# Residual rows stored ahead of the experts' sums, and the scan's states walked up and down

## The reference

```python
mod = (silu(c) @ wmod).reshape(16, 6, 1, 256)          # sa, ca, ga, sb, cb, gb
ga, gb = keep_away_from_zero(ga), keep_away_from_zero(gb)
h = layernorm(x) * (1 + ca) + sa
x = x + ga * attn(h)
h = layernorm(x) * (1 + cb) + sb
x = x + gb * ffn(h)                                    # the output

def attn(x):                                           # 512 inner channels, 16 states
    xn = layernorm(x) * norm_scale + norm_bias
    xb, z = split(xn @ W_in)
    xb = silu(conv3(xb) + conv_b)
    dt = softplus(xb @ W_dt + b_dt)
    A, B, C = -exp(A_log), xb @ W_B, xb @ W_C          # B, C: 512 tokens x 16 states
    for t in range(512):                               # for every state n
        s[:, n] = exp(dt[t] * A[:, n]) * s[:, n] + dt[t] * xb[t] * B[t, n]
        y[t] = sum over n of s[:, n] * C[t, n]
    return x + ((y + D * xb) * silu(z)) @ W_out

def ffn(x):                                            # 16 experts, 4 of them per token
    w = route(x)                                       # 512 x 16 weights, 12 of each row zero
    return sum over e of w[:, e] * (silu(x @ gate[e].T) * (x @ up[e].T)) @ down[e].T
```

## Time and profile before

| | us |
|---|---|
| median of 3 runs (2824.08 to 2827.97) | 2825.69 |
| the profiled execution, its own time | 2827.94 |
| its span, first to last instruction | 2826.1 |
| PE, DVE, POOL, ACT busy | 2394.2, 2427.1, 2238.7, 1566.2 |
| mean granted TensorE clock | 0.929 of full speed |

### The profile page before, as it was taken

The page is one execution under the profiler, slowest core; times in us unless marked ns, Lnnn a source line. Parts: engine busy times, 40 slices in busy tenths (PEclk is TensorE's granted clock), DMA queues, the critical chain, the costliest instruction groups (busy, mean ns, idle before and its releaser), DMA issues.

```text
span 2826.1 us, 29195 instructions
## 1 busy us (share of the span) xinstructions
PE 2394.2 (85%) x9004; PEld 1680.1 (59%) x9004; DVE 2427.1 (86%) x2450; ACT 1566.2 (55%) x2961; POOL 2238.7 (79%) x1563
## 2 busy tenths in 40 slices
PE   3445698998989899998989999898989989898799
PEld 1212466666756666665666667566666756566678
DVE  2678899989989898999999898998989999898932
ACT  3555666566556656655665665566565556655311
POOL 1577888888888888888888888888888888887922
PEclk7677899989989898998989899898999999999999
DMA  4699999999999999999999999998999999999921
GB/s 111 183 226 230 228 235 244 231 235 236 236 232 238 236 234 231 239 235 232 237 240 235 229 236 234 232 238 231 234 235 229 238 231 239 235 240 223 257 69 49
DMA packets 354510, 626.18 MB, mean 222 GB/s; under 512 B 51489, under 2 KB 162081, under 8 KB 354353
## 3 DMA queue, kind: packets, MB, share of 16 engines
q0 software_dynamic: 72960, 243.30, 45.3%
q1 hardware_dynamic: 281392, 381.01, 43.0%
HBM read 379.25 MB, written 10.06 MB: 138 GB/s over the span
## 4 chain that ended last, share of the span: by engine, by line
PE 40%; DVE 24%; issue 12%; POOL 8%; ACT 8%; DMA 7%; SPq 1%; DVEq 0%; POOLq 0%; ACTq 0%
DVE hbank L705 13%; PE wbank L477 13%; PE mbank L489 6%; PE wbank L419 4%; PE wbank L505 4%; PE wbank L379 4%; POOL unit L1177 4%; PE wbank L367 3%; DMA w_all<-w_scratch 2%; DMA gsum<-unit 2%; PE wbank L502 2%; DMA w_scratch<-rows_out 2%; DVE unit L719 2%; ACT z L828 2%; DVE act L683 2%
## 5 line engine op out<-in xcount | busy, mean ns | idle before, releaser
L1177 POOL TENSOR_TENSOR unit<-dtx,b_bc 128x1024 f32<-128x1024 f32 x512 | 1359.5, 2664 | 7.5 <-DMA b_bc<-bc_scratch 4.3
L705 DVE TENSOR_TENSOR_SCAN hbank<-hbank,unit 128x1024 f32<-128x1024 f32 x512 | 1173.2, 2291 | 104.0 <-ACT hbank L1007 90.7
L1007 ACT ACTIVATE hbank<-dt,a_neg 128x512 f32<-128x512 f32 x1024 | 669.0, 681 | 334.3 <-DVE unit L719 300.1
L489 PE MATMUL mbank<-down_t,act 128*128 128x256 f32 x2048 | 532.9, 400 | 60.8 <-POOL act L1145 34.4
L1189 POOL DMA_DIRECT2D gsum<-unit x448 | 451.3, 1007 | 161.9 <-DVE unit L719 74.8
L719 DVE TENSOR_TENSOR unit<-hbank,c_bc 128x1024 f32<-128x1024 f32 x448 | 545.4, 1217 | 21.7 <-DMA c_bc<-bc_scratch 1.4
L1145 POOL TENSOR_TENSOR act<-act,w_all 128x512 f32<-128x512 f32 x256 | 360.9, 1410 | 254.3 <-DVE act L683 230.9
L477 PE MATMUL wbank<-h_t,gate_t 128*128 128x256 f32 x2048 | 496.8, 386 | 24.4 <-DVE act L683 13.0
L489 PEld LDWEIGHTS mbank<-down_t,act 128*128 128x128 f32 x2048 | 399.9, 199 | 165.8 <-issue 62.3
L477 PE MATMUL wbank<-h_t,up_t 128*128 128x256 f32 x2048 | 486.9, 381 | 11.8 <-DVE gz L587 10.2
L477 PEld LDWEIGHTS wbank<-h_t,gate_t 128*128 128x128 f32 x2048 | 387.3, 192 | 128.4 <-DVE act L683 27.4
(11 more groups left out here) (121 smaller groups left out, 2394.9 us busy)
## 6 DMA issues: line engine op xcount, KB each, us to landing
gsum<-unit POOLq DMA_DIRECT2D x448, 512.0 KB, 7.6
b_bc<-bc_scratch SPq DMA_DIRECT2D x512, 256.0 KB, 6.3
c_bc<-bc_scratch SPq DMA_DIRECT2D x512, 256.0 KB, 5.6
w_all<-w_scratch SPq DMA_DIRECT2D x256, 256.0 KB, 5.0
ht<-in_L_attn_x_dram SPq DMA_DIRECT2D x16, 512.0 KB, 8.8
w_out<-in_L_attn_W_out_dram SPq DMA_DIRECT2D x16, 512.0 KB, 10.1
ht<-in_L_attn_x_dram POOLq DMA_DIRECT2D x16, 512.0 KB, 10.3
out_dram<-xt SPq DMA_DIRECT2D x16, 512.0 KB, 3.3
```

What stands on the lines that cost most here:

```text
L489: m = eng.matmul(mbank[:, u * H:(u + 1) * H], act[:, (n - 1) % MOE_RING, j, u * P:(u + 1) * P], down_t[:, e, :], start=(e == 0 and u == 0) ...
L705: eng.tensor_tensor_scan(h, h, unit[:, g % RING, :, :].rearrange("p a t -> p (a t)"), 0.0, ALU.mult, ALU.add).then_inc(scanned, 1)
L1007: eng.activation(hbank[g % HB][:, a, :], dt[:, 2 * q + a, :], ACT.Exp, scale=a_neg[:, 2 * q + a, n:n + 1]).then_inc(decayed, 1)
L1177: eng.tensor_tensor(unit[:, g % RING, :, :], dtx[:, 2 * q:2 * q + 2, :], b_bc[:, s:s + 1, :].to_broadcast([P, 2, T]), ALU.mult).then_inc(d ...
```

## The change

The row x1 is stored to the output as soon as it is there (`store_x1`, one DMA of 512 KB on SP, at moment 27 of the slot). A half's experts' sum is then only multiplied by gb, from `mbank` straight into `xt` (over x1), and POOL issues a DMA that adds this half of `xt` onto the output in DRAM (256 KB, two per row, `accum_op=ALU.add`). DVE's multiplication waits until the store of x1 has landed (`x1_out`). And the 16 states of a pair are now taken upward and downward in turn (`state_at`), with the order reversed from row to row; a row of B or C that still lies in its ring from the last units before the turn is used again and not loaded (`rows_held`).

```diff
+        def state_at(g):
+            row, pair, u = g // NU, g % NU // NS, g % NS
+            return u if (row + pair) % 2 == 0 else NS - 1 - u
+
+        def rows_held(ring):
+            slots, table = [(None, 0, -1)] * ring, []
+            for g in range(NG):
+                row, n = g // NU, state_at(g)
+                s = (n - NS * (row % 2)) % ring
+                what, loads, reader = slots[s]
+                fresh = what != (row, n)
+                slots[s] = ((row, n), loads + fresh, g)
+                table.append((s, loads + fresh, fresh, reader))
+            return table
...
-                         ("project", behind, 4, 15, 24), ("stats", behind, 5, 20, 26),
+                         ("project", behind, 4, 15, 24), ("stats", behind, 5, 20, 26), ("store_x1", behind, 1, 27, 27),
...
-                        eng.tensor_tensor(sums, sums, gb_row[:, :].rearrange("p (a h) -> p a h", a=1).to_broadcast(
-                            [P, TT // 2, H]), ALU.mult).then_inc(moe_v, 1)
-                        need.wait_ge(moe_v, 2 * row + h + 1)
-                        eng.tensor_tensor(xt[:, row % 2, tiles, :], sums, xt[:, row % 2, tiles, :],
-                                          ALU.add).then_inc(moe_out, 1)
+                        need.wait_ge(x1_out, 16 * (row + 1))
+                        eng.tensor_tensor(xt[:, row % 2, tiles, :], sums, gb_row[:, :].rearrange(
+                            "p (a h) -> p a h", a=1).to_broadcast([P, TT // 2, H]), ALU.mult).then_inc(moe_out, 1)
...
+                    for h in range(2):
+                        if s == (EP + 1, E)[h]:
+                            tiles = slice(h * TT // 2, (h + 1) * TT // 2)
+                            need.wait_ge(moe_out, 2 * row + h + 1)
+                            need.wait_ge(x1_out, 16 * (row + 1))
+                            eng.dma_start(out[row].rearrange("(t p) h -> p t h", p=P)[:, tiles, :],
+                                          xt[:, row % 2, tiles, :], accum_op=ALU.add).then_inc(row_out, 16)
...
+            def store_x1(row):
+                x1_ready(need, row)
+                eng.dma_start(out[row].rearrange("(t p) h -> p t h", p=P), xt[:, row % 2, :, :]).then_inc(x1_out, 16)
+                yield
...
             def load_b(g):
+                s, _, fresh, reader = b_rows[g]
+                if not fresh:
+                    return
...
-                    if s == E:
-                        need.wait_ge(moe_out, 2 * (row + 1))
-                        eng.dma_start(out[row].rearrange("(t p) h -> p t h", p=P),
-                                      xt[:, row % 2, :, :]).then_inc(row_out, 16)
```

More of the change, by code:

```diff
@@ L233, in build @@
         summed = [sem(f"summed{k}") for k in range(2)]
-        etanhed, weighted, down_done, moe_v, moe_out = (
-            sem(n) for n in ("etanhed", "weighted", "down_done", "moe_v", "moe_out"))
+        etanhed, weighted, down_done, moe_out, x1_out = (
+            sem(n) for n in ("etanhed", "weighted", "down_done", "moe_out", "x1_out"))
         work = Banks(wbank, [sem(f"work{k}_full") for k in range(3)], [sem(f"work{k}_free") for k in range(3)])
@@ L301, in last_streams @@
             plan = [("mix1", last, 4, 5, 5), ("project", last, 4, 6, 6),
-                    ("stats", last, 5, 6, 8), ("turn", last, 4, 16, 18), ("load_gb", last, 1, 21, 26),
+                    ("stats", last, 5, 6, 8), ("store_x1", last, 1, 10, 10), ("turn", last, 4, 16, 18), ("load_gb", last, 1, 21, 26),
                     ("pick", last, 5, 16, 16), ("weigh", last, 2, 24, 25)]
@@ L708, in times_c @@
             def times_c(g):
-                s = g % C_RING
-                need.wait_ge(c_in[s], 16 * (g // C_RING + 1))
+                s, loads, _, _ = c_rows[g]
+                need.wait_ge(c_in[s], 16 * loads)
                 need.wait_ge(scanned, g + 1)
@@ L933, in project @@
                     if row >= 2:
-                        need.wait_ge(row_out, 16 * (row - 1))
+                        need.wait_ge(row_out, 32 * (row - 1))
                         need.wait_ge(rnorm_p, 4 * (row - 1))
@@ L1002, in decay @@
                 g, a = i // 2, i % 2
-                q, n = g % NU // NS, g % NS
+                q, n = g % NU // NS, state_at(g)
                 need.wait_ge(dt_cut, g // NS + 1)
@@ L1170, in drive @@
             def drive(g):
-                row, q, s = g // NU, g % NU // NS, g % B_RING
-                need.wait_ge(b_in[s], 16 * (g // B_RING + 1))
+                row, q = g // NU, g % NU // NS
+                s, loads, _, _ = b_rows[g]
+                need.wait_ge(b_in[s], 16 * loads)
                 need.wait_ge(dtx_made, 2 * row + q + 1)
@@ L1299, in load_b @@
             def load_b(g):
+                s, _, fresh, reader = b_rows[g]
+                if not fresh:
+                    return
+                n = state_at(g)
                 need.wait_ge(bc_out, 16 * (g // NU + 1))
[L1301 to L1304, removed]
+                if reader >= 0:
+                    need.wait_ge(driven, reader + 1)
+                eng.dma_start(b_bc[:, s, :], bc_dram[g // NU, n:n + 1, :].to_broadcast([P, T])).then_inc(b_in[s], 16)
             def load_c(g):
+                s, _, fresh, reader = c_rows[g]
+                if not fresh:
+                    return
+                n = NS + state_at(g)
                 need.wait_ge(bc_out, 16 * (g // NU + 1))
-                if g >= C_RING:
-                    need.wait_ge(c_scaled, g - C_RING + 1)
-                eng.dma_start(c_bc[:, g % C_RING, :], bc_dram[g // NU, NS + g % NS:NS + g % NS + 1, :].to_broadcast(
-                    [P, T])).then_inc(c_in[g % C_RING], 16)
+                if reader >= 0:
+                    need.wait_ge(c_scaled, reader + 1)
+                eng.dma_start(c_bc[:, s, :], bc_dram[g // NU, n:n + 1, :].to_broadcast([P, T])).then_inc(c_in[s], 16)
             def load_w(row, s):
@@ L1403, in _ @@
             older.rest()
-            need.wait_ge(row_out, 16 * NB)
+            need.wait_ge(row_out, 32 * NB)
 _INS = ['L0_attn_x', 'L0_attn_norm_scale', 'L0_attn_norm_bias', 'L0_attn_W_in', 'L0_attn_conv_w', 'L0_attn_conv_b',
```

3 lines of the change are left out of this document (2 added, 1 removed).

## The result

The changed kernel takes 2837.13 us (median of 4 runs, 2834.17 to 2842.16) against 2825.69: ratio 1.0043, 95% interval 1.0028 to 1.0058. It is slower by 0.43%, where I forecast 0.2% faster; the time lies just outside my range of 2803 to 2836. The profiled execution took 2834.17 us, its span is 2832.4.

The account below looks back on a forecast made before the run. No single engine bounds it; the chain of waits runs through DVE, POOL and DMAs. Terms -8.4 + 4.0 - 3.0 + 1.4 - 1.1 + 1.0 = -6.1 us gave 2821.8, adjusted to 2819.5 against median 2825.69; range 2803 to 2836.

Parts of the forecast that it names:

- Half 1, POOL: Adding DMA's issue in POOL's gapless run: 1.1 us less 0.79 covered, +0.31 per slot, +4.0 us in 13 slots.
- the cover: Wait for w_all before POOL's weighting, 0.79 us per slot, taken to hide part of half 1's issue.
- Half 0, DVE: Removing L696 at the slot's end brings scan, next slot and PE 0.6 us forward: 14 slots, -8.4 us.
- 0 (POOL sets it instead): Lower bound of half 0's DVE saving: at DVE's hand-over to PE, POOL sets the pace and nothing is gained.
- Half 0, POOL: Adding DMA's issue ahead of the addition at 1388.21: 1.1 us hidden by POOL's idle 1.56 us, cost 0.
- SP: Output store no longer delays w_scratch's store: weights up to 3.7 us earlier, w_all's wait gone; -3.0 us in the last slot.
- The store of x1: Issued ahead of the next row's ht load, which lands 1.7 us later; counted 0, bounds 0 and +1 per slot.
- The turns: 112 fewer loads, net -50 us of engine time with the adding DMAs, over units 13 to 20; counted 0.
- Rival 4: The transfers were the bound: half of the 50 us of engine time would give 2795 us; chance 0.06.
- Last slot and tail: Earlier weights -3.0, transfer before the last gsum addition +1.4, shorter experts' chain -1.1, final adding DMA +1.0 us.
- Rival 1: POOL's issue at half 1 becomes the bound: at issue cost p = 2.0 us, 2837.5 us; chance 0.22.
- Rival 2 (the clock): PE's 1.2 GHz stretch at the weights' routing takes half 0's gain: +2.3, 2828 us; chance 0.18.

Follow-up runs that it names:

- no_add1: Changed kernel without half 1's adding DMA, its output lacking that half's gated sums; 2807.79 us, 0.9943 of the kernel before.
- one_pass: Kernel before with DVE's gating and residual passes made one, the residual left out of the output; 2826.58 us, ratio 1.0010.
- no_add0: Changed kernel without half 0's adding DMA, its output lacking that half's gated sums; 2829.85 us, 1.0023 of the kernel before.
- turns_late_out: Kernel before with state order and held rows alone, plus SP's output store moved behind w_scratch and the first w_all loads; 2806.79 us, 0.9922.
- turns: Kernel before with only the alternating state order and the held rows of B and C, output path unchanged; 2813.76 us, 0.9964.
- late_x1: Changed kernel with the store of x1 issued some 30 us later in SP's order; 2836.9 us, 1.0042 of the kernel before.
- late_both: Changed kernel with half 1's adding DMA (rows 0 to 13) and the store of x1 both issued later; 2814.97 us, 0.9966 of the kernel before.
- adds: Changed kernel with rising state order and every B and C row loaded, keeping stored residual and adding DMAs; 2834.26 us, 1.0035 of the kernel before.

## Why the prediction was wrong, step by step

**Half 1, POOL: +0.31 us a slot forecast (+4.0 in 13 slots), +1.05 measured (+13.7)**, from scan 12 to scan 18, before to after. This is the first of the two steps that failed. The issue was sized at 1.1 us between 0.9 and 1.9; its row is 1.2 to 2.1 us, and its price, in POOL's run as in the slot, 1.9 (1.93 us, scan 12 to 18, no_add1 to after). The rows of L1173 (duration ns min/median/max; idle before it; landing):

```profile
L1173 POOL DMA_DIRECT2D out_dram<-xt x32: 1202/1277/2142, 405.5 to 2826.8; - x32
...
  issue: 7.2, 12
...
DMA to landing us min/median/max: 4.4/6.0/9.6
```

And the cover was looked up on the wrong path. I set the issue against `w_all`'s wait on the way to unit 17; it reaches the scans earlier, through L1117, ACT's queue and the gates, at unit 15, where `w_all` covers nothing. With 1.9 for 1.1 my own sum gives 1.9 - 0.79 = 1.1 a slot, nearly the measured number, but by luck: by the table, what stands against the issue is DVE's saving at 12-13 (0.64), which I had at nothing, and only 0.11 at 16-17, on `w_all`'s path. The kernel before already showed ACT waiting at L834's place for L1098 in all 13 slots (14.8 us): an edge without slack, which I had not followed.

**Half 0, DVE: -0.6 us a slot forecast (-8.4 in 14), -0.07 measured (scan 28 to 4, in one_pass and after alike), and nothing in the time of one_pass.** This is the second step that failed. I took PE's wait of 1.62 us for proof that the edge was worth its 0.6. It was shortened by 0.73, and at the next edge of the same chain, POOL's weighting, PE waited 0.72 longer. The bound "0 (POOL sets it instead)" was the right one.

**Half 0, POOL: 0 forecast, 0.2% measured** (no_add0), in the tail and at half 1 of the next slot; nothing at its own place.

**SP: the mechanism was right.** The store no longer stands before `w_scratch`, the waits for `w_all` are gone, and that is worth 7 us (turns_late_out to turns, 0.4% by the ratios). In the changed kernel it hardly shows (16-17 is 0.11 us shorter, 0.54 in no_add1), since unit 15 is late before unit 17 can be early.

**The store of x1: 0 forecast, right by the result** (late_x1); 7 us once the other bound is gone (late_both). **The turns: 0 forecast**; -11.5 alone, 0 or a little more than 0 in this kernel (adds 2834.26, after 2837.13). Rival 4 was right in part: loads left out, an estimated 94 us of engine time by the prediction's price, are worth 11.5 us alone. By the Trainium skill's DMA: Bandwidth & Descriptors, section Queues, rings and completion order, a DMA engine takes the queues it has work for in turn. That fewer loads on one queue would then speed the other fits only weakly: in the turns' trace the median landing of a `gsum` addition went from 7.6 to 7.4 us, while `w_all`, on the loads' own queue, went from 5.0 to 4.5.

**Last slot and tail: -3.0 + 1.4 - 1.1 + 1.0 = -1.7 forecast, +2.5 measured** (-1.1 and +3.6). The last slot gave 1.1 us where I had SP's 3.0. In the tail +1.3 stood against +3.6. By the chains of before and after, the last `gsum` addition takes 6.9 us to land instead of 5.4, +1.5 for my +1.4; it is issued 0.8 later, counted at nothing, for of the 1.50 us that POOL idled before it 0.52 are left; the experts' chain is 0.5 shorter for my 1.1; and the end, from DVE's first instruction on the last half, is 6.6 us instead of 4.8, +1.8 for my +1.0. The last addition in the chain of waits, before, then after:

```profile
2688.71 5.36 DMA gsum<-unit
```

```profile
2692.17 6.91 DMA gsum<-unit
```

Timeline of POOL after, at the last additions and at the end:

```profile
2689.55 0.87 POOL L1217 DMA_DIRECT2D gsum<-unit  x1 [1.36 <-DMA gsum<-unit]
2690.13 1.53 POOL L1173 DMA_DIRECT2D out_dram<-xt  x1
2692.17 0.90 POOL L1217 DMA_DIRECT2D gsum<-unit  x1 [0.52 <-DMA gsum<-unit]
...
2826.81 1.21 POOL L1173 DMA_DIRECT2D out_dram<-xt  x1 [3.08 <-DVE xt L715]
```

From the last issue to the end of the span are 5.6 us. The Trainium skill's formula for a DMA that POOL issues (DMA: Bandwidth & Descriptors, section Anatomy of one DMA), quoted in the prediction, gave an estimated 2.6; the trace does not agree.

**The rivals.** Rival 1 named the mechanism, the place and a time of 2837.5 at p = 2.0 us. Both numbers came out, the time by luck: it took the path over `w_all`, its 6.2 us at half 0 were wrong, and it kept the -8.4 of DVE. I gave it 0.22 because I placed two packets per partition nearer to one than to four; the row's median, 1.28 us, lies nearer to four (1.50) than to one (0.89), and the pause ahead of it was in none of my rows. Rival 2 (the clock) is refused: it had no change, and the mean granted clock is higher after (0.934) than before (0.929) although the kernel is slower. What the filling matmuls gained was 0.16% (0.07 to 0.25%).

## What to carry to other kernels

Before an instruction is added to a queue, follow who waits for what stands behind it, all the way to the engine that sets the pace, and look in the list of waits for edges that wait every time: a microsecond there cost a full microsecond of slot here, on an engine that idles for a fifth of the span. A wait that an edit removes is a gain only if the next wait on the same chain ends earlier; look for the second-latest input before counting it. Two edits may each be worth 7 to 12 us alone and nothing behind a third that delays an earlier point of the same slot, so time them apart.

## What the runs showed of the hardware

POOL's issue of an adding DMA of 256 KB into DRAM took 1.2 to 2.1 us and 1.9 in all in a run of POOL work without a gap, where a 512 KB addition into SBUF with half the packets per partition takes 0.9. It landed after 4.4 to 9.6 us. TensorE's clock could be brought from 0.95 to 0.98 of full speed over 2130 us by matmuls in its waits, for 0.16% of the time.

One row of DVE that no edit touched got dearer: `r_w<-r_cut,r_s` of the routing took 6.1 us in 16 runs of it before, 12.1 after, 11.6 in adds and 6.9 in turns; it accounts for most of what DVE's saving fell short of. One of them in the kernel after, and the drive that POOL was then running:

```profile
2105.37 2.64 POOL L1205 TENSOR_TENSOR unit<-dtx,b_bc 128x1024 f32<-128x1024 f32 x1
...
2106.52 1.58 DVE L677 SCALAR_TENSOR_TENSOR r_w<-r_cut,r_s 128x64 f32<-128x64 f32 x1
```

All 11 long ones after (0.35 to 1.59 us) start while POOL runs L1205 and end 0.09 us after it does; the other 5 overlap it by at most 0.02 us and take 0.22. So in these traces this DVE instruction stands until POOL's drive is through, and it is dearer because it now meets the drive more often (11 times in 16, 5 before). That is read from the rows; no run changes it alone.
